# The routed parts of the last three output tiles are added on TensorE, by products with the identity

## The reference

```python
x = x + attn(layernorm(x))                 # cumulative sum of outer products, 16 heads of 16
h = layernorm(x)
w, idx = top_k(softmax(h @ Wg), 4)         # 32 experts, 4 for each row
y[row] = sum over its 4 experts of swiglu_e(h[row]) * w      # W1, W3 [32, 256, 128], W2 [32, 128, 256]
z = (silu(h @ Ws1) * (h @ Ws3)) @ Ws2      # the shared expert, 256 hidden columns
out = x + (y + z)
```

## Time and profile before

| | us |
|---|---|
| median of 3 runs | 571.62 (571.03 to 573.02) |
| profiled execution, its own time | 570.52 |
| its span in the trace | 568.8 |
| TensorE busy | 540.5 (95%) |
| VectorE busy | 360.4 (63%) |
| ScalarE busy | 367.4 (65%) |
| GpSimd busy | 331.8 (58%) |
| mean granted TensorE clock | 0.978 of full |

### The profile page before, as it was taken

One profiled execution on the slowest core, in us unless ns is written; L12 is line 12 of the kernel. 1 busy time (PEld: TensorE's weight loads), 2 busy tenths in 40 slices (PEclk: granted clock), 3 DMA queues, 4 the chain that ended last, 5 costly groups with the idle time before them and its releaser, 6 DMA issues.

```text
span 568.8 us, 17659 instructions
## 1 busy us (share of the span) xinstructions
PE 540.5 (95%) x4793; PEld 375.6 (66%) x4793; DVE 360.4 (63%) x1353; ACT 367.4 (65%) x1258; POOL 331.8 (58%) x367
## 2 busy tenths in 40 slices
PE   6899999999999998798999999999999999979996
PEld 3465666666666664366888888888888885534554
DVE  7698999999999994751333333333333336843886
ACT  3687999898999974303666666666666665643452
POOL 6010477677777777751655565565566564447991
PEclk8999999999999999797999999999999999979999
DMA  8998365555565545935777766666666654419997
GB/s 243 318 292 292 115 224 205 203 217 200 201 228 197 213 181 188 361 115 142 221 212 216 216 199 180 187 186 171 189 184 180 181 181 144 142 67 398 409 406 265
DMA packets 65085, 123.26 MB, mean 217 GB/s; under 512 B 9824, under 2 KB 44000, under 8 KB 64992
## 3 DMA queue, kind: packets, MB, share of 16 engines
q1 hardware_dynamic: 47824, 78.07, 43.5%
q0 software_dynamic: 13056, 39.86, 19.1%
q10 hardware_dynamic: 4112, 4.19, 2.2%
HBM read 58.49 MB, written 63.60 MB: 215 GB/s over the span
## 4 chain that ended last, share of the span: by engine, by line
PE 79%; issue 4%; POOL 4%; DVE 4%; SPq 3%; DMA 2%; ACT 2%; ACTq 1%; POOLq 0%; DVEq 0%
PE pS L965 20%; PE pQV L830 10%; PE pS L981 9%; PE pS L743 8%; PE pS L797 5%; PE pO L890 5%; POOL xs L471 4%; PE pQV L947 3%; PE pO L871 3%; PE pT L947 2%; PE pT L776 2%; PE pO L805 2%; SPq L389 2%; DMA xg<-xs 1%; PE pQV L759 1%
## 5 line engine op out<-in xcount | busy, mean ns | idle before, releaser
L499 POOL DMA_INDIRECT ys<-gsh,dst x144 | 138.1, 959 | 118.8 <-ACT gsh L666 99.6
L471 POOL DMA_INDIRECT xs<-xg,posi x128 | 123.8, 967 | 52.1 <-issue 31.4
L965 PE MATMUL pS<-w,after_a 128*128 x512 | 134.1, 385 | 0.0
L965 PEld LDWEIGHTS pS<-w,after_a 128*128 128x128 f32 x512 | 88.4, 193 | 7.3
L981 PE MATMUL pS<-w,after_a 128*128 x256 | 76.6, 381 | 0.0
L665 ACT CAST dst<-xg 128x1 int32 x128 | 24.5, 191 | 76.8 <-PE pS L981 75.0
L1077 DVE TENSOR_TENSOR w<-pS,tri 128x512 f32<-128x512 f32 x96 | 64.9, 677 | 1.4 <-PE pS L797 1.4
L830 PE MATMUL pQV<-w 128*128 128x512 f32 x128 | 63.3, 617 | 0.5 <-ACT w L537 0.5
L1342 DVE COPY after_a<-pT 128x128 f32<-128x128 f32 x72 | 21.0, 292 | 67.3 <-PE pT L970 67.1
L1342 DVE COPY after_a<-pO 128x128 f32<-128x128 f32 x72 | 21.0, 292 | 66.6 <-PE pO L970 65.9
L666 ACT ACTIVATE gsh<-pS,xg 128x256 f32<-128x256 f32 x128 | 60.7, 474 | 0.2 <-issue 0.2
(11 more groups left out here) (222 smaller groups left out, 1096.0 us busy)
## 6 DMA issues: line engine op xcount, KB each, us to landing
xg<-xs SPq DMA_DIRECT2D x128, 160.0 KB, 2.5
ys<-gsh SPq DMA_DIRECT2D x32, 512.0 KB
w<-ys SPq DMA_DIRECT2D x32, 512.0 KB, 15.2
w<-in_L_ffn_W ACTq DMA_DIRECT2D x1, 4096.0 KB
out<-xall SPq DMA_DIRECT2D x14, 256.0 KB, 6.3
xs<-padrow SPq DMA_DIRECT2D x32, 80.0 KB
xg<-xs SPq DMA_DIRECT2D x32, 80.0 KB, 2.2
ys<-gsh,dst POOLq DMA_INDIRECT x144
```

The source lines that it names most:

```text
L471: pool.indirect_dma_start(out=xs, out_offset=bass.IndirectOffsetOnAxis(ap=posi[:, a.r8, k:k + 1], axis=0), in_=xr[:, a.r8, :], in_offset=N ...
L499: pool.indirect_dma_start(out=ys, out_offset=bass.IndirectOffsetOnAxis(ap=dst[:, j % 8:j % 8 + 1], axis=0), in_=y[:, j % 8, :], in_offset= ...
L965: last = pe.matmul(pS[a.b][:, 0:2 * F], xgT[:, a.b, k, :], w13_of(e, k), start=(k == 0), stop=(k == KC - 1))
```

## The change

For tiles 29, 30 and 31 (`ON_PE` = 29) GpSimd's sum, ScalarE's copy and VectorE's `add_parts` go away. TensorE computes the shared expert of these tiles into a bank of their own (pS[1], pS[2], pS[3]) without closing the accumulation, and then adds the four loaded parts of each tile into the same bank, by four products with `ident` as the stationary and 256 columns of a part as the moving operand. VectorE adds the bank to `xall` with one instruction, `add_z`. The loop of `shared_z(7)` is written out for that; for tiles 29 to 31 it has no wait for VectorE, but a wait for the load of the parts ahead of their products. Tile 28 stays as it was.

```diff
--- before.py
+++ after.py
@@ -113,6 +113,8 @@
 
     assert NU == P
 
+    ON_PE = NT - 3
+
     def late(tile_of, skew):
         for whole_or_mixed, a in enumerate((tile_of(skew), tile_of(skew + 1))):
             if a is not None and mixed(a.t) == bool(whole_or_mixed):
@@ -499,7 +501,7 @@
                 pool.indirect_dma_start(out=ys, out_offset=bass.IndirectOffsetOnAxis(ap=dst[:, j % 8:j % 8 + 1], axis=0),
                                         in_=y[:, j % 8, :], in_offset=None).then_inc(y_out[j % 8], 16)
 
-            for t in range(NT):
+            for t in range(ON_PE):
                 pool.wait_ge(parts_in[t % PB], 16 * (t // PB + 1))
                 pool.tensor_tensor(parts(t)[:, 0:2, :], parts(t)[:, 0:2, :], parts(t)[:, 2:4, :], ALU.add
                                    ).then_inc(S["parts_sum"], 1)
@@ -715,9 +717,6 @@
             half_silu(7, 1)
             copy_parts(27)
             copy_parts(28)
-            copy_parts(29)
-            copy_parts(30)
-            copy_parts(31)
 
         @block.tensor
         def _(pe):
@@ -990,7 +989,23 @@
                     shared_h(g, m)
                 if g > NPRE:
                     shared_z(g - 1)
-            shared_z(NG - 1)
+            pe.wait_ge(S["gsh_done"], FC * NG)
+            for t in range(QT * (NG - 1), NT):
+                q = t % QT
+                if t < ON_PE:
+                    wait(pe, S["summed"], t - 1 - QT * LATE)
+                bank = (pQV, pO)[q % 2] if t < ON_PE else pS[q]
+                for m in range(FC):
+                    last = pe.matmul(bank[:, 0:D], gsh[:, (NG - 1) % 2, m, q * P:(q + 1) * P], ws2[:, m, :],
+                                     start=(m == 0), stop=(m == FC - 1 and t < ON_PE), skip_group_check=True)
+                if t < ON_PE:
+                    last.then_inc(S["z_ps"], 1)
+            for t in range(ON_PE, NT):
+                pe.wait_ge(parts_in[t % PB], 16 * (t // PB + 1))
+                for k in range(TOP_K):
+                    last = pe.matmul(pS[t % QT][:, 0:D], ident[:], parts(t)[:, k, :], start=False, stop=(k == TOP_K - 1),
+                                     skip_group_check=True)
+                last.then_inc(S["z_ps"], 1)
 
 
         @block.vector
@@ -1242,9 +1257,10 @@
 
             def add_z(t):
                 wait(dve, S["z_ps"], t + 1)
-                if t >= QT * LATE:
+                if QT * LATE <= t < ON_PE:
                     dve.wait_ge(S["added"], t + 1)
-                dve.tensor_tensor(xall[:, t, :], xall[:, t, :], (pQV, pO)[t % 2][:, 0:D], ALU.add
+                z = (pQV, pO)[t % 2] if t < ON_PE else pS[t % QT]
+                dve.tensor_tensor(xall[:, t, :], xall[:, t, :], z[:, 0:D], ALU.add
                                   ).then_inc(S["z_done" if t < QT * LATE else "summed"], 1)
 
             def shared_add(g):
@@ -1418,11 +1434,8 @@
             add_z(27)
             add_parts(28)
             add_z(28)
-            add_parts(29)
             add_z(29)
-            add_parts(30)
             add_z(30)
-            add_parts(31)
             add_z(31)
 
 _INS = ["L0_attn_X", "L0_attn_Wq", "L0_attn_Wv", "L0_attn_q_norm_w", "L0_attn_v_norm_w", "L0_ffn_Wg", "L0_ffn_W1",
```

## The result

| | before | after |
|---|---|---|
| median of 10 runs, us | 571.33 (569.07 to 573.38) | 573.89 (572.70 to 577.73) |
| ratio | | 1.006, 95% interval 1.0042 to 1.0079 |
| profiled execution, us | 570.52 | 575.06 |
| its span, us | 568.8 | 573.2 |

The change makes the kernel slower by 0.6%: 2.4 to 4.5 us by the interval, 2.6 us by the medians. In a later series the same kernel stood at 1.0039 (1.0019 to 1.0058), 1.1 to 3.3 us, so about 2.5 to 3 us fits both (its medians are 573.03 and 571.10, 1.9 us apart).

The account below looks back on a forecast made before the run. VectorE was taken to bound the kernel's end, TensorE after the change: -1.8 us for removed rounds and +5.2 us for 12 products give +3.4 us, median 575.0 us, range 573.2 to 576.8.

Parts of the forecast that it names:

- What bounds the end: Last tiles: VectorE sets the pace at 1.31 us a tile; after the change it waits for TensorE's products.
- What goes away is worth 1.8 us: Tail: VectorE's part additions for three tiles go; with parts costing nothing, it ends at 563.78 instead of 565.57.
- A product costs 0.43 us: TensorE behind tile 31's group: 12 identity products priced like L759, 5.19 us in an unbroken line.
- the rival at their price: TensorE's identity products cost what transposes do: 12 take 2.6 us, end moves +0.8 us to 572.4; chance 0.05.
- the one with bare weight loads: TensorE's loads of `ident` are not hidden: 12 products take 9.7 us, end moves +7.9 us to 579.5; chance 0.05.
- The estimate from the Trainium skill's figures: TensorE's products: 98 ns a pass, four passes, 0.39 us each, 4.7 us for 12; set aside for the rows.
- The waits for the parts cost nothing: TensorE ahead of each tile's products: loads land by 555.3, first product at 563.2; between 0 and 0.11 us, taken as 0.
- The last store takes 2.8 us as before: End of the span: tile 31's store finds an emptier queue, yet the same 2.8 us to landing is counted.
- The median, 575.0: Whole kernel: the median of 571.62 moves by the same 3.4 us to 575.0, or +0.6%.
- the profile's offset to the median: Whole kernel: the profiled execution before is 1.1 us below the median of the runs, 571.62.
- the stretch before 559.7 moved: Sign against the forecast: TensorE's own chain ahead of tile 28's group, at 559.71, was claimed not to change.
- VectorE would stay the bound with a product below 0.15 us: Rival for the tail: VectorE's 0.42 us rounds still bound it, time 569.8; chance 0.03, shared with drift between runs.

Follow-up runs that it names:

- the early half: Kernel before, with the first two product groups of the shared expert's group 3 no longer waiting for the last experts' rows; ratios 0.9975 and 0.9968.
- both edits: Kernel before, with GpSimd summing tiles 28 to 31 a second time and group 3's first two product groups not waiting for the last experts' rows; ratio 0.9970.
- GpSimd's second sum: Kernel before, with GpSimd making another 128x256 sum for tiles 28 to 31, so VectorE adds the parts with one instruction; ratios 0.9970 and 0.9986.
- two tiles: Changed kernel with only tiles 30 and 31 by identity products, 8 of them; ratio 1.0000 against the kernel before.

## Why the prediction was right

- **What bounds the end**: right. VectorE held it before, TensorE after, and taking either engine's work away moved the tail as expected.
- **What goes away is worth 1.8 us**: right to 0.01 us at the last addition (4.07 predicted and measured without the products). At the end of the span it is worth 1.4 us only.
- **A product costs 0.43 us**: right. The 24 records took 5.19 us, and each further tile 1.73 us. So L759, with the same shapes, was the right row, and the transposes of the earlier trace rows the wrong one: the rival at their price (tail 6.7 us) is refuted by the 9.25 us. So is the one with bare weight loads (tail 13.8 us), as the 24 loads of the same weights, 0.19 us each, stayed hidden.
- The estimate from the Trainium skill's figures in "TensorE: Matmul & The Clock Gate", section Back-to-back issue gap, was 98 ns for a pass of 256 columns, and with the four passes for true FP32 in "FP8 and Floating Point Precision", section TensorE Precision Notes, 4.7 us for the products. They took 5.19 us, which is 108 ns for a pass if there are four; the trace does not agree with 98 ns.
- **The waits for the parts cost nothing; tiles 29, 30, 31 complete 1.73 us apart; tail 9.26 us**: right, 9.25 us twice. TensorE's clock stayed at the 2.4 GHz level through the tail.
- **The last store takes 2.8 us as before**: this is the term of the sum that was mis-sized. It takes 1.7 us. I had seen that the queue would be emptier and still took the same landing time; the row that I read was that of a store behind others. This makes the loss 2.3 us in the trace from the tail's start on, instead of 3.4, and the measured medians are 2.6 us apart.
- **The median, 575.0**: measured 573.9, inside 573.2 to 576.8, so the forecast was 1.1 us too high, the size of the store's term. The lower end of the range is near: in the later series the median was 573.0. The range had made room for the products' price and for the scatter of the runs, and none for the store; that the median fell inside is owed to room made for other things. Taking the profile's offset to the median as fixed was good to about 1 us; the stages ahead of the closing one start it anywhere between 507.1 and 511.6 on one chip.
- **"I would be wrong if the stretch before 559.7 moved"**: it did move, by 2.1 us, in the first profile. The sign was badly chosen. From the start of the closing stage to the tail it was 52.00 us before (507.71 to 559.71), and 52.14 and 51.14 us in the two profiles of the changed kernel; what moved is the stage's start, which scatters.
- **VectorE would stay the bound with a product below 0.15 us**: a slip on which nothing rests. At 0.15 us the 12 products cost the 1.8 us that go away; to hold VectorE's rounds of 0.42 us, a tile's four products would have to take less than that together, 0.105 us each.

## What to carry to other kernels

When work is moved from the engine that ends last to one that would be next, take both sums: what the first gives back, down to where the second takes over (1.8 us here), and what the second then pays in full (5.2 us). The work was moved to the one engine with none to spare, while GpSimd sat idle for the last 12 us and could take a part without lengthening the tail. And what ends after the last instruction, a store, has a price that depends on what is queued ahead of it, at its issue as well as on its way: gains at the end shrink there and losses too. Before an engine is made to finish earlier, read how full the DMA engines are behind it.

## What the runs showed of the hardware

- A float32 product by the identity cost what L759's products of its shape cost, 0.432 us: two records, 0.216 us apart at 256 columns. The 24 and 32 loads of the same identity in a row were all made, 0.19 us each, and all stayed hidden. Two transposes by the same identity in the earlier trace rows were 0.11 us apart for 128 columns.
- A 128 KB store landed 1.7 us after its issue with an empty queue and 2.1 to 3.6 us behind others. Its issue took SyncE 0.33 us with an empty queue, and 0.43 to 0.46 us for the last two in the early half, behind a queue that had not paused for 9 us.
- In every kernel with the 1.7 us of idle time at the seam of the stages, the granted clock was at the 1.2 GHz level over 3 to 6 us of the work behind it: the 32 records there took 15.54 to 17.04 us in these profiles, 14.00 us in both of the early half. The idle time is not needed for the fall: with both edits there was none (15.17 us), and there, as in the second profile of GpSimd's second sum, the clock fell while the last expert records were running. With both edits TensorE was busy for 0.73 of the 2 us before the fall (623 to 625); in the early half it was busy for 0.77 of the same stretch (618 to 620), and the clock did not fall. What decides it, these runs don't show.
- In the series in which the kernel before took 677 to 685 us the first stage ended at 312 to 318 us instead of 229 to 231 (TensorE's last product of `mask` and `tri`, with two tiles, both edits and the early half, against the kernel before and the changed one). All engines were less busy between 60 and 310 us, with waits that the profile could not name, while the closing stage's records were unchanged. Its cause is not known.
